# QKV weights held on chip by row blocks, and a first stage of eight tiles at a time, in an eight-core attention and feed-forward kernel

## What is computed

```python
qkv = x @ Wqkv.T                      # x: (2048, 1024) on each core, Wqkv: (3072, 1024)
q, k, v = split(qkv); k = k / 8
# per head, for t = 0 .. 2047
state = g * state + outer(v[t], k[t])  # 64 x 64
y[t] = state @ q[t]
x1 = layernorm(x + y @ Wout.T)
h = silu(x1 @ w1.T) * (x1 @ w2.T)      # 4096 wide
h = gelu(h @ h1.T); h = gelu(h @ h2.T) # 4096 x 4096 each
out = layernorm(x1 + h @ w3.T)
```

## Time and profile before

| | |
|---|---|
| three runs, us | 3107.86, 2841.47, 2854.01 (median 2854.01) |
| profiled execution, us | 2842.7 |
| its span on the slowest core (3), us | 2841.2 |
| spans of the eight cores, us | 2837.6 to 2841.2 |
| mean granted TensorE clock of the cores | 0.992 to 0.993 |
| PE's busy tenths in 40 slices of the span | 5 7, then thirty-seven times 9, then 7 |
| busy share: PE, VectorE, ScalarE, POOL | 97%, 13%, 15%, 5% |
| read from memory, written on chip by DMA | 441.31 MB, 235.73 MB |

### The profile page before, as it was taken

How to read it: one execution, slowest core, us unless ns; L and a number is a source line. 1 busy time by engine, 2 the same in 40 slices (tenths; PEclk the granted TensorE clock), 3 DMA queues, 4 the chain that set the end, 5 groups by cost and what they waited for, 6 DMA issues and landing times.

```text
span 2841.2 us, 31537 instructions; the slowest of 8 cores (2837.6 to 2841.2 us)
## 1 busy us (share of the span) xinstructions
PE 2769.3 (97%) x13568; PEld 1259.3 (44%) x13568; DVE 380.4 (13%) x562; ACT 431.1 (15%) x627; POOL 128.2 (5%) x243
## 2 busy tenths in 40 slices
PE   5799999999999999999999999999999999999997
PEld 2344444444444444444444444444444444444443
DVE  3355653200000000000001143100000000000004
ACT  2232333110010010001000232100100010010011
POOL 1000000000000000000000000000000000000000
PEclk9899999999999999999999999999999999999998
DMA  9935344464444444444444355644444444444441
GB/s 172 166 72 108 68 75 75 74 100 79 79 77 75 74 75 78 78 80 77 75 75 67 62 101 105 97 79 79 78 76 75 74 76 78 78 79 76 75 75 60
DMA packets 47784, 235.73 MB, mean 83 GB/s; under 512 B 4896, under 2 KB 9120, under 8 KB 26016
## 3 DMA queue, kind: packets, MB, share of 16 engines
q0 software_dynamic: 38000, 216.02, 47.8%
q1 hardware_dynamic: 9648, 17.69, 2.1%
HBM read 441.31 MB, written 8.39 MB: 158 GB/s over the span
## 4 chain that ended last, share of the span: by engine, by line
PE 96%; DMA 3%; issue 0%; DVE 0%; ACT 0%; POOL 0%; DVEq 0%; ACTq 0%; POOLq 0%
PE PS L375 70%; PE PS L365 16%; PE PS L337 3%; PE PS L343 2%; DMA PB<-wvr 2%; PE PS L352 2%; PE PS L357 1%; DMA PB<-wqk 1%; PE PS L414 1%; PE PS L411 1%; PE PS L385 0%; PE PS L397 0%; PE PS L426 0%; ACT X1T L668 0%; DVE R L524 0%
## 5 line engine op out<-in xcount | busy, mean ns | idle before, releaser
L375 PE MATMUL PS<-R,PB 128*128 128x512 bf16 x8960 | 1934.4, 379 | 0.0
L375 PEld LDWEIGHTS PS<-R,PB 128*128 128x128 bf16 x8960 | 876.8, 98 | 1057.1
L365 PE MATMUL PS<-X1T,PB 128*128 128x512 bf16 x2048 | 444.9, 379 | 0.0
L661 ACT ACTIVATE R<-PS,CFS 128x512 bf16<-128x512 f32 x256 | 175.9, 687 | 1577.1 <-PE PS L375 1577.0
L365 PEld LDWEIGHTS PS<-X1T,PB 128*128 128x128 bf16 x2048 | 199.6, 98 | 239.7
L510 DVE SCALAR_TENSOR_TENSOR R<-PS,CFS,X1T 128x512 f32<-128x512 f32 x32 | 24.0, 751 | 1959.5 <-PE PS L375 1959.5
L337 PE MATMUL PS<-X1T,PB 128*128 128x512 bf16 x512 | 120.2, 389 | 26.7 <-DMA PB<-wqk 26.7
L505 DVE SCALAR_TENSOR_TENSOR R<-PS,CFS,TMPA 128x512 bf16<-128x512 f32 x128 | 96.1, 751 | 295.0 <-PE PS L365 274.9
L653 ACT ACTIVATE TMPA<-PS,CFS 128x512 f32<-128x512 f32 x128 | 87.7, 687 | 315.1 <-PE PS L365 315.0
L337 PEld LDWEIGHTS PS<-X1T,PB 128*128 128x128 bf16 x512 | 48.6, 99 | 85.7 <-issue 33.3
L343 PE MATMUL PS<-PB,X1T 128*128 128x512 bf16 x256 | 60.9, 394 | 17.1 <-DMA PB<-wvr 17.1
(11 more groups left out here) (63 smaller groups left out, 563.2 us busy)
## 6 DMA issues: line engine op xcount, KB each, us to landing
PB<-h1p POOLq DMA_DIRECT2D x64, 1024.0 KB, 9.9
PB<-h2p POOLq DMA_DIRECT2D x64, 1024.0 KB, 9.9
PB<-w POOLq DMA_DIRECT2D x64, 512.0 KB, 5.7
PB<-wqk POOLq DMA_DIRECT2D x15, 1024.0 KB, 25.0
PB<-w3p POOLq DMA_DIRECT2D x12, 1024.0 KB, 9.8
R<-xT SPq DMA_DIRECT2D x32, 256.0 KB, 7.3
PB<-wvr POOLq DMA_DIRECT2D x8, 1024.0 KB, 15.7
yT<-R SPq DMA_DIRECT2D x32, 256.0 KB, 3.0
```

The source lines that it names most:

```text
L365: mm = t.matmul(bank, PB[panels_of(tl)[0] % 4][:, o:o + 128], xs(2 * tb + th, c), start=(c == 0), stop=(c == 7))
L375: mm = t.matmul(bank, pb[:, c * 128:c * 128 + 128], h1b(c, th) if kind == "h2" else ub(c, th), start=(c == 0), stop=(c == 31))
L661: s.activation(h1b(ot, th) if kind == "h1" else ub(ot, th), bank, AF.Gelu, scale=cf("s1h" if kind == "h1" else "s2h", ot, 1)).then_inc(don ...
```

## The change

What it does, by parts:

- **Weights in memory** are given as `wT` (1024 x 3072) and `outT` (1024 x 1024), the transposed matrices, and are loaded by blocks of 128 rows (input features) instead of by output panels.
- **Queries' and keys' weights** go once into PB, which is now one tensor of 4 MiB, and stay there until `("qk", 3, 15)` is done; only then do the feed-forward panels use PB, as before.
- **Values' and output weights** (2 MiB each) share R1's slot `w2`. The values' weights come first, for windows 0 and 1. Then, each load waiting for the last tile that uses what lies there: output, values (window 2), output, values (window 3), output.
- **First round.** The 24 tiles of window 0 are made in three rounds of eight tiles on all eight banks (`PRE_BANK`): values, queries, keys. In a round the loop over the 8 row blocks is outside and that over the eight tiles inside, so that a pass of eight matmuls needs one block. Each value block is one transfer of x (128 KB) and one of weights (256 KB), each query and key block 512 KB for two passes.
- **Tile order.** In a window, values of w+1 come before queries and keys in w = 0; in w = 1 and 2 one query tile, the `op` tiles, the other queries, the statistics, then values and keys. In w = 1 and 2 one tile (`LEAD`) runs ahead of the window's first scores, and the third chunk ends with 9 tiles, the fourth with 8.
- **Evictions.** Of window 0's query and key tiles, ScalarE takes the odd ones, after its tables. VectorE evicts the 8 values first, then makes its copies and mask.
- **Other queues.** SP's `vb` waits for the fourth value block, and the residual rows for the 24th tile.

```diff
-FILLS = [[(2, 1, 2, 1)] * 4] + [[(2, 2, 2, 2), (2, 2, 2, 2), (3, 2, 2, 2), (3, 2, 2, 2)]] * 3
+LEAD = (0, 1, 1, 0)
+FILLS = [[(2, 1, 2, 1)] * 4,
+         [(2, 2, 2, 2), (2, 2, 2, 2), (3, 2, 2, 2), (2, 2, 2, 2)],
+         [(2, 2, 2, 2), (2, 2, 2, 2), (3, 2, 2, 2), (2, 2, 2, 2)],
+         [(2, 2, 2, 2), (2, 2, 2, 2), (3, 2, 2, 2), (3, 2, 2, 2)]]
+PRE = 24
+PRE_BANK = (3, 4, 7, 0, 1, 2, 5, 6)
...
-    tiles = qkv_tiles(0)
+    tiles = v_tiles(0) + q_tiles(0) + k_tiles(0)
...
         if w == 0:
-            tiles += qkv_tiles(1)
-            continue
-        rest = qkv_tiles(w + 1) if w + 1 < NW else u0[:24]
-        step = [("op", w - 1, oc) for oc in range(8)] + rest
-        step[16:16] = [("lm", w - 1), ("lq", w - 1)]
-        tiles += step
+            tiles += v_tiles(1) + q_tiles(1) + k_tiles(1)
+        elif w + 1 < NW:
+            q = q_tiles(w + 1)
+            tiles += q[:1] + op + q[1:] + stat + v_tiles(w + 1) + k_tiles(w + 1)
+        else:
+            tiles += op + u0[:8] + stat + u0[8:24]
...
+            q.wait_ge(d_xv[3], 32)
             q.dma_start(out=TMPA[:], in_=vb).then_inc(d_vb, 16)
-            q.wait_ge(p_dn, 1)
+            q.wait_ge(p_dn, PRE)
...
-            load_x(0)
-            g.dma_start(out=PB[0][:, 0:1024], in_=wqk[0][:, 0:1024]).then_inc(d_w0, 16)
-            g.dma_start(out=PB[0][:, 1024:4096], in_=wqk[0][:, 1024:4096]).then_inc(d_wt[0], 16)
-            for k in range(1, 24):
...
+            wv = wTr[:, :, 2048:3072]
+            for c in range(8):
+                g.dma_start(out=xs(0, c), in_=xTr[:, c, 0:TW]).then_inc(d_xv[c], 16)
+                g.dma_start(out=w2(c, 0, 1024), in_=wv[:, c, :]).then_inc(d_xv[c], 16)
+            for i, done in ((0, d_q), (1, d_k)):
+                for j in range(4):
+                    o = i * 8192 + j * 2048
+                    g.dma_start(out=PB[:, o:o + 2048].rearrange("p (c o) -> p c o", c=2),
+                                in_=wTr[:, 2 * j:2 * j + 2, i * 1024:(i + 1) * 1024]).then_inc(done[j], 16)
+            for j in range(2):
+                g.dma_start(out=X1T[:, 4096 + j * 2048:4096 + (j + 1) * 2048].rearrange("p (c t) -> p c t", c=4),
+                            in_=xTr[:, 4 * j:4 * j + 4, TW:2 * TW]).then_inc(d_x1[j], 16)
+            load_x(2)
+            g.wait_ge(p_dn, AT[("v", 1, 7)] + 1)
+            load_w2(outTr, d_ow)
+            load_x(3)
+            for w in (2, 3):
+                g.wait_ge(p_dn, AT[("op", w - 2, 7)] + 1)
+                load_w2(wv, d_vw)
+                g.wait_ge(p_dn, AT[("v", w, 7)] + 1)
+                load_w2(outTr, d_ow)
...
+            def first_round(r):
+                for c in range(8):
+                    if r == 0:
+                        t.wait_ge(d_xv[c], 32)
+                    elif c % 2 == 0:
+                        t.wait_ge((d_q, d_k)[r - 1][c // 2], 16)
+                    for i in range(8):
+                        d = r * 8 + i
+                        bank = PS[BANK[d]][:]
+                        if c == 0 and r > 0:
+                            t.wait_ge(ev[BANK[d]], USE[d])
+                        if r == 0:
+                            mm = t.matmul(bank, xs(0, c)[:, (i // 2) * 128:(i // 2) * 128 + 128],
+                                          w2(c, (i % 2) * 512, 512), start=(c == 0), stop=(c == 7),
+                                          skip_group_check=True)
+                        else:
+                            mm = t.matmul(bank, qkwt(r * 8 - 8 + i, c), xs(0, c), start=(c == 0), stop=(c == 7),
+                                          skip_group_check=True)
+                        if c == 7:
+                            mm.then_inc(p_dn, 1)
...
-                if kind == "qk" and tl[1] == 0:
+                if kind == "qk" and tl[1] == 0 and tl[2] % 2 == 0:
```

More of the change, by code:

```diff
@@ L286, in _ @@
-            load_x(0)
-            g.dma_start(out=PB[0][:, 0:1024], in_=wqk[0][:, 0:1024]).then_inc(d_w0, 16)
-            g.dma_start(out=PB[0][:, 1024:4096], in_=wqk[0][:, 1024:4096]).then_inc(d_wt[0], 16)
-            for k in range(1, 24):
-                w, i = k // 6, k % 6
-                panel(k, wqk[i] if i < 4 else wvr[i - 4])
-                if k == 5:
-                    load_x(1)
-                if k == 7:
-                    for i in range(2):
-                        g.dma_start(out=R1a[:, 16384 + i * 4096: 16384 + (i + 1) * 4096], in_=outw[i]).then_inc(d_ow, 16)
-                if k == 9:
-                    load_x(2)
-                    load_x(3)
+                g.dma_start(out=PB[:, (k % 4) * 4096:(k % 4) * 4096 + n], in_=src).then_inc(d_wt[k % 4], 16)
@@ L393, in ktrans @@
                     t.wait_ge(d_cb, 16)
+                    for i in range(4, 8):
+                        t.wait_ge(*evac(AT[("qk", 0, 8 + i)]))
                 else:
@@ L565, in _ @@
             v.wait_ge(d_cf, 16)
-            for d in range(16):
+            v.wait_ge(d_vb, 16)
+            for d in range(8):
                 dense_out(d)
@@ L586, in _ @@
                     ln = w > 0
+                    if cl == 0:
+                        for d in range(d, d + LEAD[w]):
+                            dense_out(d)
+                        d = STEP0[w] + LEAD[w]
                     qscale(c)
@@ L636, in dense_out @@
                 done = ev[BANK[d]]
[L637 removed]
+                if kind == "qk" and (tl[1] > 0 or tl[2] % 2 == 1):
                     w, ot = tl[1], tl[2]
@@ L705, in _ @@
             s.copy(sbt(0), SF).then_inc(s_sb, 1)
+            for d in range(8, PRE):
+                dense_out(d)
             for w in range(NW):
```

120 lines of the change are left out of this document (62 added, 58 removed).

## The result

The changed kernel takes 2821.4 us (median of four runs, 2820.0 to 3064.9), before it was 2854.7 us (four runs, 2841.5 to 3107.9). The ratio is 0.9912, 95% interval 0.9884 to 0.9941: a gain of 0.6 to 1.2%, within 2%. Some runs are longer at a lower granted clock: those of over 3000 us, which the ratio leaves out, and some of before at 2853.8 to 2860.1 us (four of the 14 that ran beside the experiments and that are compared; the other ten took 2840.9 to 2843.7), which it counts, and in which two or four cores had a mean clock near 0.984 instead of 0.992. So the medians are 33.3 us apart, but the two profiled executions 2842.7 - 2820.0 = 22.7 us, and the sum of the prediction was made against the first of these. The prediction was 2811.0 us and a gain of 31.7 us, 9 us too many. Its range from 2800 to 2834 holds the result; the narrower one, 2804 to 2817 with a chance of 66%, does not.

A forecast was written before the change was run, and what follows sets the result against it. Bytes were taken to bound the kernel before 133 us, then PE. Start 14.4 plus window 0 20.0 less 2.7 in windows 1 and 2 gave 31.7 us, so 2842.7 became 2811.0; range 2800 to 2834, 66% for 2804 to 2817.

The forecast's parts named there:

- What bounds the kernel, and window 0: Before 133 us bytes bound, then PE; with weights on chip window 0 takes 60.3 instead of 80.3 us, 20.0 gained.
- The value round: Start, window 0's values: first matmul about 8 us, eighth block landed 28.5, last pass ended 30.2.
- a landing is seen later than its bytes: Start: a block's landing is seen 2.3 us after its bytes moved, putting the eighth value block at 28.5 us, not 26.2.
- The clock in the start: Value passes: 1.75 us each taken, 3.4 at low clock left open; low clock expected only after long idle time.
- Queries and keys: Start, second and third rounds: first query pass ends 34.1 us, keys 60.7; window 0 starts at 61.7 instead of 76.05.
- another of the signs named: Start: matmuls of the second and third round (queries, keys) waiting for weights would show the forecast wrong.
- Issuing: Start, POOL's queue: issuing costs nothing; up to 1.03 us per issue, two smaller ones run ahead of 2.5 us blocks.
- Windows 1 and 2: The new tile order within these windows costs 2.7 us: -1.6 -2.4 +1.3.
- the three mechanisms: Windows 1 and 2: statistics wait 0.8 us each, mask wait 1.1 to 1.2 each; lead tile hides 1.27 in window 2.
- The shared slot: Windows 1 to 3: value and output weight loads expose 0 to 2.5 us each; 0 taken.
- Fixed cost of each transfer: Rival, 3%: 2.4 us per transfer not overlapped, 15 more transfers, start 40 us later than before, 2865 us.
- the late start: Rival, 17%: low-clock value passes or short rows at 135 GB/s; value blocks 32.0, start 67.6 us (+5.9), time 2820.

The follow-up runs named there:

- held run: Changed kernel with query and key blocks issued only once the eighth value block has landed: 2825.1 us.
- run with x in two pieces: Changed kernel plus later statistics tile, later layer-norm blocks, output weights loaded in halves, and window 0's x as two 512 KB transfers: 2808.8 us, ratio 0.9858.
- three removals together: Changed kernel with statistics tile and layer-norm blocks 4 and 5 later, output weights in halves, first x as two 512 KB transfers: 2808.8 us, ratio 0.9858.
- the two edits: Changed kernel, windows 1 and 2: statistics tile behind third chunk's scores and transposes, layer-norm blocks 4 and 5 moved into fourth chunk: 2817.9 us, ratio 0.9905.
- the split: Kernel with later statistics tile and layer-norm blocks, plus the 2 MB output-weight load cut into two 1 MB column halves: 2812.9 us, ratio 0.9872.

## Why the prediction was right and where it was not

- **What bounds the kernel, and window 0**: right. With the weights on chip the four chunks take 60.2 us (60.3 predicted), and none of them waits for a DMA or for VectorE. VectorE's six more evictions in the chunk cost nothing.
- **The value round**: the first matmul was predicted at 8 us and starts at 9.3 (core 3) to 11.0 (core 5); the end of the last pass was predicted at 30.2 and is seen at 34.8 (36.0 on core 7). The eighth block at 32.95 us is over the 32 that the prediction itself had named as a sign of being wrong. The step that failed is "a landing is seen later than its bytes", 2.3 us, taken from one panel of before with few transfers around it. It measured 5.2 us. The held run (at most 1.0) and the run with x in two pieces (1.9) point to two causes, what is queued behind and how many transfers there are. The bytes themselves were 1.5 us late as well (95 and 132 GB/s in the first two stretches instead of 116 and 162). Together they are 4.4 of the 4.7 us that the start lacks.
- **The clock in the start**: left open between 1.75 and 3.4 us a pass. On core 3 three passes ran at the lower speed: the first (3.57), the second (the 8.91 us of the 32 matmuls from 14.33 on are 3.57 for eight and 5.34 for 24), and the seventh (3.41, behind a wait of 3.07 us); the other five took 1.89 or less. On core 7 the last was one (3.12, behind 2.49 us). For the first two passes the stretches view gives a granted clock of 1.00 all the same, for the seventh 0.50. The Trainium skill ("TensorE: Matmul & The Clock Gate", HAM oscillation) describes a loop in which every pass behind a DMA wait, there of about 3 to 5 us, runs at 1.2 GHz. Of the eight passes of core 3, the later seven behind waits of at most 3.1 us, the rows show three at that speed. A wait of 3.80 us on core 0 left the next pass at 1.89.
- **Queries and keys**: right but for the later start. The last value eviction lets the first pass end at 38.4, and the other fifteen take 26.6 us without a wait, where the sum had 26.6 (34.1 to 60.7) too. The first query block, predicted at 31.4, came at 36.26 on core 3, and PE waited 1.43 us for it, another of the signs named; as the evictions ended later still, it cost nothing. The other weight blocks are ahead of need.
- **Issuing**: "costs nothing" was taken from one issue of 1.03 us. POOL was busy for 16.8 of the first 24 us (3.9 before). No run shows that this delayed a byte, and none excludes that it is the cost of each transfer.
- **Windows 1 and 2**: the three mechanisms are there, in the predicted places, and their sizes are +1.1 (not 0.8), 1.67 (not 1.2) and -1.3: 4.3 us instead of 2.7. In both chains the times of hand-over were missing, 0.33 us from PE's end to ScalarE's start and 0.47 us from VectorE's end to PE's restart. The larger error is what was not in the sum at all: behind these waits the clock fell to the lower level and took 1.72 us each time. The prediction had read this for the first tile after 18.6 us idle, and had concluded that only long idle time does it; waits of 1.67 to 3.06 us do it as well, though not each time, and the trace of before already had one behind 1.94 us (the row at 277.24). Four times on core 7 make 6.9 us, on core 3 3.4 us more than before. Waits and clock give 11.2 and 7.7 us, and 10.2 and 6.9 were measured; about 1 us of it is left unassigned on both.
- **The shared slot**: predicted at 0, and in the changed kernel it was 0 on seven cores and 0.5 us on core 3, so there was no slack: once either stall was shortened the output weights were late by up to 2.5 us, the upper end given. The stalls had covered the load.
- **Fixed cost of each transfer**: the rival that decides from 1.6 us each on was rejected, and that was right; but it is not nothing. The Trainium skill ("DMA: Bandwidth & Descriptors", Anatomy of one DMA) puts about 2.0 us on each. Passes 2 to 5 of core 3, with two transfers each, end within 8.9 us, which excludes 2.0 us one after another; the run with x in two pieces puts an estimated 0.5 us on each.
- **The rivals**: the late start (17%) is what happened, with blocks at 32.9 (32.0 in its text) and the start 5 us late (5.9). Its two reasons were not the main ones: the low clock in some passes, the last of cores 1 and 7 aside, did not set the end of the round, and slower bytes make 1.5 us of it. Its time of 2820 is the measured one, but partly by luck, since the low clock of windows 1 and 2 makes up as much as the start.

The three removals together give 33.4 us on core 3 where the forecast had 31.7. That the wait for the statistics is still 2.17 us there, with its low clock, says that up to 3.9 us (2.17 and 1.72) are left in each of the two windows; this was not tried.

## What to carry to other kernels

Where a first stage is bound by bytes and its consumer works block by block, send as few and as large transfers as still let the consumer start early: here two halves of x beat both eight pieces and one. When a wait is costed, add the hand-over between engines (0.1 to 0.5 us here) and the possible fall of PE's clock behind it, 1.7 us for waits of the sizes seen here. And when a stall is removed, look at which load was finishing under it: a shortened wait may show little in the time until that load is split. Here the two edits gave 3.6 us together, and 8.6 with the split.
